# Attention: value products in two pairs a slot, key tiles 2 and 3 added into key tile 1 on GpSimd for the softmax denominator

## The chip, the cores and the metric

The kernel runs on one core of one Trainium2 chip. The metric is the device time of one execution in microseconds (us). The program is one launch of one decoder layer.

## What is computed

The input `x` is 4 sequences of 512 tokens, 512 wide, in float32. The layer has three parts, each followed by a residual sum and a layer norm: causal self-attention, a choice of one of four experts by token number, and a mixture of eight experts with a shared one. The change lies in the attention:

```
qkv = x @ w_attn + b_attn              # 16 heads of 32
att = softmax(causal(q k^T / sqrt(32)))
y   = (att @ v) @ w_proj + b_proj
x   = layernorm(x + y)
```

The softmax is divided at the end: the kernel keeps exp(score - rowmax), sums it over the keys, and multiplies the value product by the reciprocal of that sum.

## The kernel before

`attention_phase` treats 16 groups, 4 for each of the 4 sequences; a group g is four heads. All engines walk through one list of steps that `attention_steps` writes out by hand (line 24 on); each engine takes from it the kinds that concern it, in the list's order. So the list sets the order on TensorE (PE), GpSimd (POOL), ScalarE (ACT), VectorE (DVE) and SP alike. A pass of the loop over `s` (line 46) does the second half of group s, the first half of group s+1, the Q and K products of group s+2, and the value products of group s-1.

The steps, by their kind:

- Q, K, V, PR: products of the projections, each in three parts of four 128x128 by 512 matmuls (line 471), into one of two banks of `psT`. XT transposes x (line 485), CW transposes the weights of the next phase (line 492).
- The high and low halves of Q and K (`ch_hi`, ScalarE, line 613; `ch_lo`, VectorE, line 738) are stacked into `qS` and `kS` by 24 DMAs a group, nearly all from SP (line 354). ScalarE writes the next `ch_hi` of Q only when all stacks of the earlier groups have landed (line 612).
- P1 (line 537): scores of a unit, 10 units a group, two banks of `psS`; VectorE adds the mask and takes the row maximum (line 754). P1 of unit n waits for the maximum of unit n-2.
- M (line 545) turns the maxima into the layout of the exponent step.
- P2 (line 558): the scores transposed, keys on the partitions, less the maximum; ScalarE's exponential (line 641) writes unit u to `p_f[:, u, :]`, and GpSimd clears what is above the diagonal (`affine_select`, line 413). A unit is 512 columns. Units 0 to 3 hold key tile 0 of the four heads, units 4 to 7 key tile 1 (queries 128 to 511, 384 columns) and key tile 3 (queries 384 to 511, the last 128 columns), units 8 and 9 key tile 2 (256 columns for each head).
- PV(g, j) (line 562): for key tile j, four matmuls with the values into `psO` (one for each head, 32 columns of weights, beside each other in the array) and four with ones into `psN`, for the denominator. Both accumulate over j, in the order 0, 1, 3, 2. `pv_done` counts the tiles. A float32 matmul has two records in the trace.
- NORM (line 757): VectorE transposes `psN`, takes the reciprocal, transposes back and multiplies with `psO`. YH splits the result on ScalarE (line 648) and GpSimd (line 418).
- LN1 and LN2 (lines 433, 805) are the layer norm, ST the scatter to `sorted_x1` from GpSimd (line 441), LZ the load of the next z (line 448) and ZB its bias addition on GpSimd (line 427). LZ waits for all scatters so far (line 447).

In a pass, after Q, K and three P1, the loop of line 79 writes for each j: PV(s-1, j), one P1, one P2, and in the second pass of each sequence one of two XT. The rest of P1 and P2 follows, with the V or PR products spread between them. ScalarE's exponential of units 0, 4 and 8 waits until PV has read what it overwrites (line 640):

```
if u in (0, 4, 8) and g:
    act.wait_ge(pv_done, QT * (g - 1) + {0: 1, 4: 3, 8: 4}[u])
```

Of the kernel before, what the change touches and what calls it, by code (L numbers as in the profile page):

```python
# [13 lines left out]
ALU = mybir.AluOpType  # L14
# [3 lines left out]
P = 128  # L18
EPS = 1e-5
ONE = 1  # L20
BELOW_ALL = -1e30


def attention_steps(B, QT, NG):
# [13 lines left out]
    steps = []  # L38
# [7 lines left out]
    for s in range(NG):  # L46
        b, at = s // 4, s % 4
        fill, early, soon = [], [], []
# [3 lines left out]
        if at == 1:  # L52
# [3 lines left out]
            early = turn[:2]  # L56
# [16 lines left out]
        if not head:  # L73
            steps += p1[:2] + [("M", s)]
            p1 = p1[2:]
        else:
            p1 = p1[3:]
        if s:
            for n, j in enumerate(order):
                steps += [("PV", s - 1, j)] + p1[n:n + 1] + p2[n:n + 1] + early[n:n + 1]  # L80
                if s == NG - 2 and n < 2:
                    for i in (2 * n, 2 * n + 1):
                        steps += [("LN2", b - 1, i), ("ST", b - 1, i)]
                if s == NG - 1:
                    steps += [("ZB", b, n)]
                if n == 1 and at == 3 and b and b < B - 1:
                    steps += [("LZ", b)]
            p1, p2 = p1[4:], p2[4:]
        p2 = [x for pair in zip(p1, p2) for x in pair] + p2[len(p1):]
# [31 lines left out]
def attention_phase(nc, sems, acc, store, ident, powm, xs_in, pos, table, x, w_attn, b_attn, w_proj, b_proj, tokens, ctx_w, sorted_x1, sorted_x2):  # L121
# [28 lines left out]
    for s in steps:  # L150
        if s[0] in ("XT", "CW") or (s[0] in ("Q", "K") and s[-1] == 2):
            hi_order[s[:-1] if s[0] in ("Q", "K") else s] = len(hi_order)

    def first(s):
# [27 lines left out]
    with ExitStack() as ctx:  # L182
# [3 lines left out]
        def sem(name):  # L186
            return sems.enter_context(nc.semaphore(f"attn_{name}"))
# [87 lines left out]
        mask_done = sem("mask_done")  # L275
        pv_done = sem("pv_done")
        flip_done = sem("flip_done")
        norm_done = sem("norm_done")
# [93 lines left out]
        def _(pool):  # L372
# [32 lines left out]
            for s in steps:  # L405
                kind = s[0]
                if kind == "P2":
# [5 lines left out]
                    pool.affine_select(out=at, in_=at, compare_op=ALU.is_ge, fill=drop, base=0,  # L413
                                       pattern=[[0, at.shape[1]], [1, P]], channel_multiplier=-1).then_inc(mask_done, 1)
                elif kind == "YH":
                    g = s[1]
# [34 lines left out]
        def _(pe):  # L451
# [22 lines left out]
            for s in steps:  # L474
# [86 lines left out]
                elif kind == "PV":  # L561
# [3 lines left out]
                    if j == 0:  # L565
# [4 lines left out]
                        if g % 4 == 0:  # L570
                            for i in range(QT):
                                pe.wait_ge(sh_free[bank_of["V", g // 4, i]], use_of["V", g // 4, i] + 1)
                    for to, values in ((psO, lambda i: v_f[:, j, (g % 4) * P + i * D:(g % 4) * P + (i + 1) * D]), (psN, lambda i: ones[:])):
                        for i in range(4):
                            u, c0 = E_AT[j, i]
                            last = pe.matmul(to[i * D:(i + 1) * D, j * P:T], values(i), p_f[:, u, c0:c0 + (QT - j) * P],  # L576
                                             start=(j == 0), stop=(j == 2), tile_position=(0, i * D))
                    last.then_inc(pv_done, 1)

        @block.scalar  # L580
        def _(act):
# [3 lines left out]
            for s in steps:  # L585
# [47 lines left out]
                elif kind == "P2":  # L633
# [3 lines left out]
                    if u == 0 and g == 0:  # L637
                        act.wait_ge(w_lo_done, 5)
                    if u in (0, 4, 8) and g:
                        act.wait_ge(pv_done, QT * (g - 1) + {0: 1, 4: 3, 8: 4}[u])  # L640
                    act.activation(p_f[:, u, :], psE[:, n % 2, :], ACT.Exp, scale=SCALE).then_inc(exp_done, 1)  # L641
# [13 lines left out]
        def _(dve):  # L655
# [11 lines left out]
            for s in steps:  # L667
# [89 lines left out]
                elif kind == "NORM":  # L757
                    g, part = s[1:]
                    if part == 0:
                        dve.wait_ge(pv_done, QT * (g + 1))  # L760
                        dve.transpose(flip, psN[:]).then_inc(flip_done, 1)
# [10 lines left out]
                elif kind == "NH":  # L772
# [4 lines left out]
                    if half == 0:  # L777
                        dve.wait_ge(pv_done, QT * (g + 1))
                        dve.wait_ge(yl_done, g)
# [1193 lines left out]
```

## Time and profile before

| what | us |
|---|---|
| median of 3 runs | 1280.78 |
| lowest and highest of them | 1274.82 and 1282.97 |
| the profiled execution | 1269.57 |
| its span | 1267.7 |
| TensorE busy in it | 1183.1 (93%) |
| VectorE busy | 686.9 (54%) |
| ScalarE busy | 456.2 (36%) |
| GpSimd busy | 240.8 (19%) |

The durations of the rows come from the profiled execution; the 1.9 us between its time and its span lie around the first and last instruction. The attention takes the first third of the span, to about 450 us. Busy time of TensorE is counted from the start of a matmul to its modelled end, and matmuls overlap; the distance from one start to the next is what a matmul costs.

### The profile page before, as it was taken

Reading aid. Unit: us, or ns where it says so; the run is one execution under the profiler, and the core shown is the slowest. Engines: PE = TensorE matmul, PEld = TensorE weight load, DVE = VectorE, ACT = ScalarE, POOL = GpSimd, SP = SyncE. Lnnn points to the kernel's source line nnn. Section 1 sums busy time; section 2 is a strip of 40 time slices with the busy share of each in tenths; the row PEclk is TensorE's granted clock in tenths of the full one; section 3 lists DMA queues with packets and bytes.
Section 4 is the critical chain, followed back from the end, with each engine's and each line's share of the span. In section 5 each row is a group of like instructions: output and inputs, shape, how many; then the busy total and the mean of one; then the engine's idle time right before and its main releaser. Section 6 shows DMA issues by size and latency. Waiting matters only on the chain.

```text
span 1267.7 us, 20196 instructions
## 1 busy us (share of the span) xinstructions
PE 1183.1 (93%) x6404; PEld 935.7 (74%) x6404; DVE 686.9 (54%) x1469; ACT 456.2 (36%) x699; POOL 240.8 (19%) x370
## 2 busy tenths in 40 slices
PE   7788999999999879994999999999999999999996
PEld 5565676576575558883688888899999997778885
DVE  5564656656557546664447634343444442666744
ACT  3254435334435322222343334244444433333331
POOL 2021314413414410003100440000000000433200
PEclk8989999999999979997999999999999999999998
DMA  7336573532524222225223666245345531666440
GB/s 241 86 100 238 179 249 118 133 88 51 150 61 125 80 85 83 84 76 157 101 82 93 208 227 199 79 149 175 122 145 172 171 99 53 206 178 195 144 139 33
DMA packets 129277, 169.72 MB, mean 134 GB/s; under 512 B 17553, under 2 KB 70801, under 8 KB 129169
## 3 DMA queue, kind: packets, MB, share of 16 engines
q1 hardware_dynamic: 115360, 136.64, 35.2%
q0 software_dynamic: 8496, 28.32, 6.7%
q10 hardware_dynamic: 5312, 3.42, 1.2%
q8 instruction: 56, 0.92, 0.3%
q14 instruction: 53, 0.43, 0.1%
HBM read 95.98 MB, written 47.19 MB: 113 GB/s over the span
## 4 chain that ended last, share of the span: by engine, by line
PE 74%; DVE 8%; SPq 5%; POOL 3%; DMA 3%; issue 3%; ACT 2%; ACTq 1%; POOLq 0%; DVEq 0%
PE routed_ps L819 18%; PE routed_ps L1370 16%; PE psT L471 11%; SPq L354 5%; PE chosen_psG L819 4%; PE chosen_psY L819 4%; PE routed_ps L1389 2%; PE routed_ps L1390 2%; PE routed_ps L1391 2%; PE psS L537 2%; PE psO L576 2%; POOL routed_rows_io L1308 2%; PE psN L576 2%; PE psE L558 2%; PE routed_ps L1411 1%
## 5 line engine op out<-in xcount | busy, mean ns | idle before, releaser
L471 PE MATMUL psT<-store 128*128 128x512 f32 x576 | 157.2, 408 | 5.4 <-DVE store L685 3.5
L754 DVE CUSTOM_DVE_ANT_0 psS<-psS,attn_mask 128x512 f32<-128x512 f32 (+3 forms) x256 | 120.8, 510 | 60.3 <-PE psS L537 60.3
L641 ACT ACTIVATE acc<-psE 128x512 f32<-128x512 f32 x160 | 93.7, 599 | 141.7 <-PE psE L558 138.2
L1370 PE MATMUL routed_ps<-routed_later,routed_held 128*128 128x512 f32 x528 | 127.3, 398 | 3.6 <-issue 2.9
L1370 PE MATMUL routed_ps<-routed_first,routed_held 128*128 128x512 f32 x528 | 128.0, 396 | 1.4 <-DVE routed_first L1809 1.4
L471 PEld LDWEIGHTS psT<-store 128*128 128x128 f32 x576 | 105.7, 195 | 25.1 <-issue 4.0
L1370 PEld LDWEIGHTS routed_ps<-routed_later,routed_held 128*128 128x128 f32 x528 | 100.5, 192 | 28.0 <-DVE routed_held L1713 3.5
L819 PE MATMUL routed_ps<-routed_held,routed_h_hi 128*128 x624 | 116.1, 328 | 0.5 <-DVE routed_h_lo L1754 0.3
L1370 PEld LDWEIGHTS routed_ps<-routed_first,routed_held 128*128 128x128 f32 x528 | 99.7, 191 | 22.2 <-DVE routed_first L1809 1.8
L1308 POOL DMA_INDIRECT routed_rows_io<-sorted_y,routed_pos x32 | 37.6, 1175 | 387.8 <-DMA sorted_y<-routed_rows_io 314.0
L413 POOL TENSOR_SCALAR_AFFINE_SELECT acc<-acc 128x256 f32<-128x256 f32 (+1 forms) x160 | 57.2, 365 | 274.0 <-ACT acc L641 273.7
L819 PEld LDWEIGHTS routed_ps<-routed_held,routed_h_hi 128*128 128x128 f32 x624 | 100.4, 188 | 1.5 <-issue 1.3
L819 PE MATMUL routed_ps<-routed_first 128*128 x351 | 91.3, 404 | 0.0
L537 PE MATMUL psS<-attn_kS,attn_qS 96*128 96x512 f32 (+3 forms) x256 | 74.0, 352 | 12.2 <-DMA attn_kS<-attn_ch_hi 4.7
L537 PEld LDWEIGHTS psS<-attn_kS,attn_qS 96*128 96x128 f32 x256 | 44.6, 195 | 53.3 <-issue 22.8
L819 PEld LDWEIGHTS routed_ps<-routed_first 128*128 128x128 f32 x351 | 63.6, 190 | 12.2
L558 PE MATMUL psE<-attn_qS,attn_kS 100*128 100x512 f32 (+3 forms) x256 | 70.1, 339 | 2.2 <-ACT acc L641 2.1
L1713 DVE TENSOR_TENSOR routed_held<-routed_sraw,routed_held 128x1024 fp32r<-128x1024 f32 x44 | 53.8, 1222 | 29.5 <-ACT routed_held L1496 29.1
L1389 PE MATMUL routed_ps<-routed_held,routed_h_hi 128*128 128x512 f32 x176 | 68.8, 391 | 0.2 <-DVE routed_h_lo L1729 0.2
L1391 PE MATMUL routed_ps<-routed_held,routed_h_lo 128*128 128x512 f32 x176 | 68.5, 389 | 0.0
L1390 PE MATMUL routed_ps<-routed_held,routed_h_hi 128*128 128x512 f32 x176 | 68.5, 389 | 0.0
L1509 ACT ACTIVATE routed_h_f<-routed_ps 128x512 f32<-128x512 f32 x44 | 26.3, 598 | 115.1 <-PE routed_ps L1370 115.1
(249 smaller groups left out, 1973.8 us busy)
## 6 DMA issues: line engine op xcount, KB each, us to landing
sorted_x<-attn_zero SPq DMA_DIRECT2D x19, 768.0 KB, 5.9
routed_sraw<-in_L_ffn_Sg_dram SPq DMA_DIRECT2D x44, 256.0 KB, 3.1
routed_sraw<-in_L_ffn_Su_dram SPq DMA_DIRECT2D x44, 256.0 KB, 3.5
routed_sraw<-in_L_ffn_Sd_dram SPq DMA_DIRECT2D x44, 256.0 KB, 4.0
routed_rows_io<-sorted_x SPq DMA_DIRECT2D x39, 256.0 KB, 3.0
sorted_y<-routed_rows_io SPq DMA_DIRECT2D x39, 256.0 KB, 2.3
attn_qS<-attn_ch_hi SPq DMA_DIRECT2D x128, 64.0 KB
attn_kS<-attn_ch_hi SPq DMA_DIRECT2D x112, 64.0 KB
```

The lines of the kernel that those rows point to most:

```text
L354: sp.dma_start(dst[r * D:(r + 1) * D, i, :].bitcast(F32), part[i * D:(i + 1) * D, qk, :].bitcast(F32)).then_inc(stack_in, 16)
L471: last = pe.matmul(out, lhs[a](k), rhs[c](k), start=(s[-1] == 0 and k == 0), stop=(s[-1] == 2 and k == KC - 1))
L537: last = pe.matmul(psS[:, n % 2, c0:c0 + (t + 1) * P], q[0:AUX, i, t * P:(t + 1) * P], k[0:AUX, i, 0:(t + 1) * P], start=True, stop=True)
L558: last = pe.matmul(psE[:, n % 2, c0:c0 + (QT - j) * P], k[0:AUX + 4, i, j * P:(j + 1) * P], q[0:AUX + 4, i, j * P:T], start=True, stop=True)
L641: act.activation(p_f[:, u, :], psE[:, n % 2, :], ACT.Exp, scale=SCALE).then_inc(exp_done, 1)
L754: last = dve.tensor_tensor_reduce(scores, scores, mask[:, (3 - t) * P:T], 1.0, BELOW_ALL, ALU.add, ALU.max, rowmax[:, g % 2, t, i:i + 1])
L819: last = pe.matmul(out, lhs[a](k), rhs[c](k), start=(n == 0), stop=(n == 3 * chunks - 1))
L1308: pool.indirect_dma_start(out=got[:, n % 4, :], out_offset=None, in_=sorted_y, in_offset=bass.IndirectOffsetOnAxis(ap=pos[k][:, t:t + 1], ...
L1370: last = pe.matmul(out, w[:, slot, at + k * P:at + (k + 1) * P], x_part(k), start=(g == 0 and k == 0), stop=(g == 2 and k == KC - 1))
L1389: pe.matmul(s_y[i], h[0], w[0], start=(c == 0), stop=False)
L1390: pe.matmul(s_y[i], h[0], w[1], start=False, stop=False)
L1391: last = pe.matmul(s_y[i], h[1], w[0], start=False, stop=(c == CH - 1))
```

## The change

In the passes s = 1 to 14 (groups 0 to 13) the order changes: one more P1 goes first, PV of tiles 0 and 1 follow each other, then come four pairs of P2 and P1, then PV of tiles 3 and 2. Tiles 1, 3 and 2 have no matmuls with ones of their own any more. GpSimd adds tile 3 and then tile 2 into tile 1, in place, where their queries meet (AD 0 and AD 1), and one set of four matmuls with ones over the 384 columns of the sum (RS) accumulates it into `psN`. AD waits until PV has read tile 1, RS waits for both AD. The exponential of unit 4 waits for RS. Groups 14 and 15 stay as they were.

```diff
+def in_pairs(g, NG):
+    return g < NG - 2
...
+        joined = s and in_pairs(s - 1, NG)
+        if joined:
+            steps += p1[:1] + [("PV", s - 1, 0), ("PV", s - 1, 1), ("AD", s - 1, 0)]
+            p1 = p1[1:]
         if s:
             for n, j in enumerate(order):
-                steps += [("PV", s - 1, j)] + p1[n:n + 1] + p2[n:n + 1] + early[n:n + 1]
+                if joined:
+                    steps += p2[n:n + 1] + ([("AD", s - 1, 1)] if n == 0 else []) + p1[n:n + 1] + early[n:n + 1]
+                else:
+                    steps += [("PV", s - 1, j)] + p1[n:n + 1] + p2[n:n + 1] + early[n:n + 1]
...
+            if joined:
+                steps += [("PV", s - 1, 3), ("PV", s - 1, 2), ("RS", s - 1)]
             p1, p2 = p1[4:], p2[4:]
...
+    def pv_before(g):
+        return sum(QT + in_pairs(n, NG) for n in range(g))
+
+    def pv_all(g):
+        return pv_before(g + 1)
...
+                elif kind == "AD":
+                    g, part = s[1:]
+                    pool.wait_ge(pv_done, pv_before(g) + 2)
+                    if part == 0:
+                        pool.wait_ge(mask_done, UNITS * g + 8)
+                        at, more_p = p_f[:, 4:8, 2 * P:3 * P], p_f[:, 4:8, 3 * P:T]
+                    else:
+                        pool.wait_ge(mask_done, UNITS * (g + 1))
+                        pool.wait_ge(sum_done, 2 * g + 1)
+                        at, more_p = p_f[:, 4:8, P:3 * P], p_f[:, 8:10, :].rearrange("p u (h n) -> p (u h) n", h=2)
+                    pool.tensor_tensor(at, at, more_p, ALU.add).then_inc(sum_done, 1)
...
-                    for to, values in ((psO, lambda i: v_f[:, j, (g % 4) * P + i * D:(g % 4) * P + (i + 1) * D]), (psN, lambda i: ones[:])):
+                    kinds = [(psO, lambda i: v_f[:, j, (g % 4) * P + i * D:(g % 4) * P + (i + 1) * D]), (psN, lambda i: ones[:])]
+                    for to, values in kinds[:1] if in_pairs(g, NG) and j else kinds:
...
+                elif kind == "RS":
+                    g = s[1]
+                    pe.wait_ge(sum_done, 2 * (g + 1))
+                    for i in range(4):
+                        last = pe.matmul(psN[i * D:(i + 1) * D, P:T], ones[:], p_f[:, 4 + i, 0:3 * P], start=False, stop=True, tile_position=(0, i * D))
                     last.then_inc(pv_done, 1)
...
-                    if u in (0, 4, 8) and g:
-                        act.wait_ge(pv_done, QT * (g - 1) + {0: 1, 4: 3, 8: 4}[u])
+                    if u in (0, 4) and g and in_pairs(g - 1, NG):
+                        act.wait_ge(pv_done, pv_all(g - 1) if u else pv_before(g - 1) + 1)
+                    elif u in (0, 4, 8) and g and not in_pairs(g - 1, NG):
+                        act.wait_ge(pv_done, pv_before(g - 1) + {0: 1, 4: 3, 8: 4}[u])
...
-                        dve.wait_ge(pv_done, QT * (g + 1))
+                        dve.wait_ge(pv_done, pv_all(g))
```

## Rows read from the trace of the kernel before

**Rows 1.** Table of stretches: us; PE, PEld, DVE, ACT, POOL busy (count); PEclk, DMA share, GB/s
```profile
171.04:202.35 31.31, 30.11 (x193) 21.73 (x196) 20.52 (x58) 11.57 (x19) 6.96 (x15) 1.00 0.53 169
...
221.38:241.08 19.70, 17.94 (x129) 10.96 (x132) 11.34 (x38) 9.52 (x15) 11.70 (x20) 1.00 0.58 160
```
**Rows 2.** Timeline of SP's queue in slots 1 and 7: start us, us, what
```profile
93.02 3.74 SPq L324 DMA_DIRECT2D sorted_x<-attn_zero  x4
97.14 7.15 SPq L354 DMA_DIRECT2D attn_qS<-attn_ch_hi  x8
...
218.53 4.96 SPq L354 DMA_DIRECT2D attn_qS<-attn_ch_hi  x8
```
**Rows 3.** Chain of waits in slots 7 and 15: start us, us, what
```profile
233.12 3.44 DMA attn_kS<-attn_ch_hi
...
408.97 5.96 DMA attn_z<-in_x_dram
```
**Rows 4.** Timeline of TensorE in slot 8
```profile
241.01 1.07 PE L576 MATMUL psO<-acc 128*32 128x512 f32 x8
...
242.87 0.50 PE L537 MATMUL psS<-attn_kS,attn_qS 96*128 96x512 f32 x1
243.20 0.40 PE L558 MATMUL psE<-attn_qS,attn_kS 100*128 100x512 f32 x1
243.53 0.85 PE L576 MATMUL psO<-acc 128*32 128x384 f32 x8
244.20 0.83 PE L576 MATMUL psN<-acc,attn_ones 128*32 128x384 f32 x8
244.96 0.51 PE L537 MATMUL psS<-attn_kS,attn_qS 96*128 96x384 f32 x2
...
245.68 0.42 PE L576 MATMUL psO<-acc 128*32 128x128 f32 x8
245.92 0.40 PE L576 MATMUL psN<-acc,attn_ones 128*32 128x128 f32 x8
246.25 0.50 PE L537 MATMUL psS<-attn_kS,attn_qS 96*128 96x384 f32 x2
...
246.97 0.64 PE L576 MATMUL psO<-acc 128*32 128x256 f32 x8
247.43 0.61 PE L576 MATMUL psN<-acc,attn_ones 128*32 128x256 f32 x8
247.97 0.50 PE L537 MATMUL psS<-attn_kS,attn_qS 96*128 96x384 f32 x2
...
248.87 0.44 PE L471 MATMUL psT<-store 128*128 128x512 f32 x1
```
**Rows 5.** Groups of GpSimd's instructions, 60 to 430 us: busy us, mean ns, idle before
```profile
L413 POOL TENSOR_SCALAR_AFFINE_SELECT acc<-acc 128x256 f32<-128x256 f32 x96 | 38.3, 410 | 89.0 <-ACT acc L641 88.8
L427 POOL TENSOR_TENSOR attn_z<-attn_z,attn_bp 128x512 f32<-128x512 f32 x16 | 20.1, 1281 | 3.8 <-DMA attn_z<-in_x_dram 3.8
...
L413 POOL TENSOR_SCALAR_AFFINE_SELECT acc<-acc 128x128 f32<-128x128 f32 x64 | 18.9, 297 | 185.1 <-ACT acc L641 184.9
...
L433 POOL TENSOR_TENSOR attn_rstd<-attn_veps,powm 128x1 f32<-128x1 f32 x12 | 6.5, 550 | 1.4 <-DVE attn_veps L801 1.4
```
**Rows 6.** Timeline of GpSimd in slot 8
```profile
244.30 0.29 POOL L413 TENSOR_SCALAR_AFFINE_SELECT acc<-acc 128x128 f32<-128x128 f32 x1 [2.83 <-ACT acc L641]
```
**Rows 7.** Timeline of TensorE in slot 1
```profile
81.61 0.60 PE L485 MATMUL psT<-ident,attn_x_in 128*128 128x128 f32 x4
82.14 0.85 PE L576 MATMUL psO<-acc 128*32 128x384 f32 x8
```
**Rows 8.** Timeline of all engines in slot 14
```profile
393.44 1.27 POOL L418 TENSOR_TENSOR attn_yT_lo<-acc,attn_yT_hi 128x512 fp32r<-128x512 f32 x1
...
398.65 0.45 PE L558 MATMUL psE<-attn_qS,attn_kS 100*128 100x384 f32 x2
```
**Rows 9.** The operations of line 805: ns min/median/max, first and last start
```profile
L805 DVE TENSOR_SCALAR attn_z<-attn_z,attn_mv,attn_rstd x16: 528/542/1516, 215.0 to 443.8; 128x512 f32<-128x512 f32 x16
```

More of the change, by code:

```diff
@@ L276, in attention_phase @@
         pv_done = sem("pv_done")
+        sum_done = sem("sum_done")
         flip_done = sem("flip_done")
@@ L577, in _ @@
                                              start=(j == 0), stop=(j == 2), tile_position=(0, i * D))
+                    last.then_inc(pv_done, 1)
+                elif kind == "RS":
[3 more added lines that the diff above has]
+                        last = pe.matmul(psN[i * D:(i + 1) * D, P:T], ones[:], p_f[:, 4 + i, 0:3 * P], start=False, stop=True, tile_position=(0, i * D))
                     last.then_inc(pv_done, 1)
@@ L777, in _ @@
                     if half == 0:
-                        dve.wait_ge(pv_done, QT * (g + 1))
+                        dve.wait_ge(pv_done, pv_all(g))
                         dve.wait_ge(yl_done, g)
```

## Prediction

> **What bounds the kernel now.** I read the page first, then the table of stretches over the attention's slots, then the chain of waits and the queue of SP, and last the timeline of one slot. I call "slot s" the time from the first value product of group s-1 to that of group s; the change touches slots 1 to 14. The busy shares of the page are sums over stages with different limits, so the table of stretches decides: it parts the slots into two kinds [rows 1]. Slot 5 lasts 31.31 us and TensorE has 193 matmul records in it: it carries the fill (output projection, input transposes; slots 4, 8, 12 carry the V product). Slot 7 lasts 19.70 us with 129 records and no fill. The reader is to see that both show a granted clock of 1.00, so the difference is work, not clock.
>
> Slots without fill are not set by TensorE. SP issues the 24 stacking DMAs of a group one by one: eight of them take 4.96 us from 218.53 [rows 2], 0.62 each, so 24 take about 15 us; then the last one lands 3.44 us after 233.12 [rows 3], and only then may ScalarE write the next `ch_hi`. 15 + 3.4 + about 1.5 for `ch_hi` and `ch_lo` is the 19.7 us of slot 7. In the chain of waits this queue holds slots 2, 3 and 7, and likewise 11. Slots 6 and 10, in which the chain comes through VectorE's normalising at about the time the stack lands, I count with them. What TensorE saves there ends in a wait for the stack. So TensorE's time counts in slots 1, 4, 5, 8, 9, 12, 13 and 14 only: 8 of 14.
>
> **What is removed and added on TensorE.** The timeline of slot 8 gives each step by the distance of starts [rows 4]. Value product 0 (values and ones) takes 1.86 (241.01 to 242.87). Value product 1: values 0.67, ones 0.76. Product 3: values 0.24, ones 0.33. Product 2: values 0.46, ones 0.54. From the first to the first fill at 248.87 are 7.86 us, with five score steps (P1) and four exponent steps (P2) between. Removed are the ones of products 1, 3 and 2: 0.76 + 0.33 + 0.54 = 1.63. Added is RS, four products over 384 columns, the form of the ones of product 1: 0.76. Net 0.87 less in a slot, and the same P1 and P2. Without any wait a slot's section would end at 7.86 - 0.87 = 6.99, and RS would start at 6.23. Over 14 slots that would be 12.2 us; over the eight that count 7.0.
>
> **What is added on GpSimd, and the wait.** AD 0 adds 4x128 elements (512 a partition), AD 1 adds 4x256 (1024). The only GpSimd addition of two SBUF tiles here is that of z and the bias, 512 elements in 1281 ns [rows 5]. I take 1.28 for AD 0 and 2.5 for AD 1, 3.8 together, since it is the same operation on the same type. From below: at the slope of the masks, (410 - 297)/128 = 0.88 ns an element on a fixed 0.18 [rows 5], they would be 0.63 and 1.08, and RS would not wait. From above: the power of one element a partition takes 550 ns [rows 5]; if each of the four separate blocks paid that anew, each AD would grow by 1.65. The value taken is that of the nearest row; no row shows an addition in blocks.
>
> Timed from the slot's start: P1 goes ahead (0.33), product 0 to 2.19, the values of product 1 have ended at 2.19 + 0.85 = 3.04 [rows 4], AD 0 runs to 4.35. P2 of unit 0 starts at 2.86; its mask can start 1.10 later (243.20 to 244.30 [rows 4, 6]), so it is ready at 3.96 and waits for AD 0: to 4.65. AD 1 stands behind it in GpSimd's queue: to 7.15. RS is wanted at 6.23. TensorE, which works in order, waits 0.9 us and ends at 7.15 + 0.76 = 7.91 against 7.86 before. The whole saving is given back as a wait. Queued behind RS are P1 of unit 8 and P2 of unit 4, and ScalarE's exponent of unit 4, which would be 0.1 later; masks 1 to 3 behind AD 1 are not wanted before the next slot.
>
> By the Trainium skill, "GPSIMD Engine Reference", part on the measured `tensor_tensor` add, 2048 elements take 4497 ns; an estimate of 2.25 us for AD 1 from it would make this wait 0.65 instead of 0.9, 0.25 us a slot better. No row here has a GpSimd add longer than 512.
>
> **Slot by slot.** Slots 4, 8, 12, 13: +0.05 each, +0.2. Slots 5 and 9 have two transposes of x between the pairs (each 0.53 from start to start, 81.61 to 82.14 [rows 7]): RS is then wanted at 6.23 + 1.06 = 7.29, after AD 1 has ended, and the full 0.87 stays: -1.7. Slot 1 has them too, but its saving ends at SP: the clears occupy it until 93.02 + 3.74 = 96.76, and the next stacking DMA went out at 97.14 [rows 2], so at most 0.38 is gained: -0.35. The slots that SP holds: 0, and a saving's cover gone costs nothing there, as the extra wait is zero to 0.1. The normalisation (DVE) starts after one more maximum than before but has one less behind it: 0.
>
> Slot 14 is different. GpSimd's queue has the one-element powers and YH ahead of AD 0; YH starts at 393.44 and takes 1.27 [rows 8]. AD 0 is then 394.71 to 395.99, the mask to 396.3, AD 1 to 398.8, RS to 399.55. Before, the same work (through P1 of unit 6) was done at 398.65 [rows 8]. That is +0.9, and here the path goes on through YH to the load of z at 408.97 [rows 3], for which the last group's masks wait. Behind AD 1 on GpSimd stand the four scatters of x1 too (ST), which the load of z waits for; they go out later by at most the two adds, 3.8 us. Four scatters and the masks between them stood before between YH's end at 394.71 and the load at 408.97, mostly waiting for ScalarE's exponents, so I cost the delay at nothing; without that cover it is 1 to 3 us. In slots 7 and 11 GpSimd's load of z leaves up to 2 us later, and so do the bias additions behind it; the masks that stand behind those are of units 7 to 9 and are wanted by product 1 of the next slot at the earliest: 0, and up to 1 us each if the load lands late.
>
> Also in slot 14 VectorE's four normalising operations L805 (median 542 ns, longest 1516 [rows 9]) stand beside AD. The longest one is that beside YH at 393.44. I cost them at nothing: at worst one more is lengthened by 1516 - 542 = 0.97 us. The Trainium skill ("SBUF — State Buffer", section "Who interferes with whom") says that VectorE in a two-port mode and GpSimd lock each other out for a whole instruction; the lengthened operation agrees. By that rule the sum would be 1 us higher, all of it in slot 14, since a maximum reads only one operand from SBUF.
>
> Sum: -0.35 - 1.7 + 0.2 + 0.9 = -0.95, rounded -1.0 us. Durations come from the execution of 1269.57 us (span 1267.7 and 1.9 around it), which becomes 1268.6. The median of the runs shown is 1280.78, 0.9% above that execution; I carry the difference over: 1279.8.
>
> **Rivals.**
> 1. The additions are fast enough and RS never waits. For it: no GpSimd add in blocks of this form is shown. Against: 1281 ns for 512 elements. AD 1 would have to end by 6.23, so both adds in 2.9 us (6.23 - 3.04 - the mask's 0.3). Then slots 4, 5, 8, 9, 12, 13 gain 0.87 each, slot 1 0.35, slot 14 about 0: -5.6, 1275.2.
> 2. GpSimd becomes the bound and the kernel gets slower. One mechanism: AD 1 ends later, TensorE stands at RS. Each microsecond more in the two adds costs one in slots 4, 8, 12, 13 and 14 and, past 0.14, in 1, 5 and 9, so the sum turns positive where they take over 4.0 us together. With 1 us more: 4 x 1.05 + 0 in slots 1, 5 and 9 + 1.9, and 0 to 3 for the late scatters in slot 14: +6 to +9, say 1288. With the upper bound for blocks (3.3 us more): 4 x 3.35 + 3 x 2.3 + 4.2, and 2.5 each in slots 6 and 10, where the chain through VectorE would then come last: about +29, 1310. Against both is that the nearest row needs no block's price.
> 3. The queue of SP does not bound and all 14 slots gain: -12, 1268.8. Against it are the 3.44 us landing row and the 15 us of issue.
> 4. The time in RS is not the 0.76 of its form, or the tighter P1/P2 row makes VectorE's maxima the bound. P1 and P2 follow at 0.72 a pair (244.96 to 245.68), before and after; by up to 0.3 a slot, +2: 1283.
>
> **How the numbers follow.** Forecast 0.52, rival 1 0.16, rival 2 0.17 (0.05 of it the extreme), rival 3 0.04, rival 4 0.11. The predicted time is the forecast's, 1279.8. The range covers rivals 1, 3, 4 and the mild form of 2, with the scatter of the runs: 1268 to 1290; the forecast alone has 1276 to 1284. About 1% (12.8 us) is what a measurement of this kernel can tell from no change. Faster by over 1% needs rival 3 with luck: 0.05. Slower by over 1% needs the extreme of rival 2 or part of it: 0.08. Same: 0.87.
>
> **What would show it.** AD 0 near 1.28 and AD 1 near 2.5 us. TensorE idle before RS by 0.5 to 1.2 us, released by GpSimd, in slots 4, 8, 12, 13, about 2 in slot 14 and none in 1, 5 and 9. Slots 4 and 8 unchanged in length, slot 5 at 30.4, slot 7 at 19.7. In a slot, psN then has the matmuls of product 0 and of RS only: two forms instead of four. Wrong if RS finds its sum done in slots 4 and 8 (rival 1), if a stretch without fill gets shorter (rival 3), or if an AD 1 takes over 3 us (rival 2).

## The result, and the profile after

The changed kernel takes 1284.58 us in the median of 18 runs (1281.11 to 1289.77), the one before, in 18 runs beside it, 1276.8 (1267.97 to 1284.29). The ratio is 1.0052 with a 95% interval of 1.0035 to 1.0069: slower by half a percent, some 6.6 us. Forecast was 1.0 us less. The time lies within the range, and within 1% of before; the change was not neutral, though, and the mechanism that slows it stands in none of the terms.

The profiled execution took 1287.56 us. Its page, part 1 (busy time of each engine):

```profile
span 1285.7 us, 19790 instructions
...
PE 1180.5 (92%) x6180; PEld 936.9 (73%) x6180; DVE 685.6 (53%) x1469; ACT 455.0 (35%) x699; POOL 288.2 (22%) x398
```

TensorE is busy 2.6 us less and GpSimd 47 us more than before. Neither tells where the time went. The parts that the prediction priced come first. GpSimd's groups, 60 to 430 us, as [rows 5]:

```profile
L445 POOL TENSOR_TENSOR acc<-acc 128x1024 f32<-128x1024 f32 x14 | 33.4, 2385 | 0.0
...
L445 POOL TENSOR_TENSOR acc<-acc 128x512 f32<-128x512 f32 x14 | 17.9, 1281 | 75.3 <-PE psO L608 75.3
```

AD 0 takes 1.28 us, as the addition of z and the bias does, so four separate blocks cost nothing beyond their elements; AD 1 takes 2.39. All products of RS stand in the list of those who waited for the additions (us, times):

```profile
  PE psN L615: 3.6, 10
```

TensorE's matmuls of RS waited 3.6 us in 10 of 14 slots, 0.36 each: in none of slots 1, 5 and 9, as forecast, and not in slot 14 either, where about 2 us were. The timeline of TensorE in slot 6 shows why it is less than the 0.9 forecast (the last column is idle time before the instruction and what ended it):

```profile
207.67 0.51 PE L589 MATMUL psE<-attn_qS,attn_kS 100*128 100x512 f32 x1
...
208.53 0.45 PE L589 MATMUL psE<-attn_qS,attn_kS 100*128 100x512 f32 x1
...
209.38 0.86 PE L608 MATMUL psO<-acc 128*32 128x128 f32 x16
210.60 0.85 PE L615 MATMUL psN<-acc,attn_ones 128*32 128x384 f32 x8 [0.36 <-POOL acc L445]
```

The pairs of P2 and P1 follow at 0.86 and 0.85 us (207.67, 208.53, 209.38), not at the 0.72 of before (244.96 to 245.68 [rows 4]), so RS is wanted some 0.4 later than I timed it, and less is left to wait for. Experiment 3, which has no additions, shows the same 0.86, and 0.67 from the values of tiles 3 and 2 to RS, where this timeline has 1.22 (209.38 to 210.60): the wait costs 0.55 in a slot, of which the row shows 0.36 as idle.

The table of stretches, as [rows 1]: slots 4, 5 and 6, then slot 7 up to the transposes of its maxima and its end, then slots 13, 14 and 15.

```profile
145.51:173.66 28.15, 27.33 (x157) 19.64 (x156) 13.90 (x42) 9.70 (x15) 8.36 (x13) 1.00 0.65 213
173.66:203.98 30.32, 28.83 (x174) 21.35 (x173) 20.21 (x58) 11.47 (x19) 10.38 (x17) 1.00 0.53 174
203.98:222.97 18.99, 17.14 (x109) 10.54 (x108) 13.91 (x42) 9.39 (x15) 11.27 (x14) 1.00 0.42 114
222.97:240.18 17.21, 14.07 (x94) 8.29 (x93) 9.74 (x35) 7.17 (x13) 12.02 (x17) 1.00 0.60 170
240.18:244.85 4.67, 4.67 (x15) 3.38 (x15) 1.37 (x4) 2.23 (x2) 3.10 (x5) 0.63 0.34 84
374.42:398.45 24.03, 21.77 (x133) 15.10 (x132) 16.62 (x52) 8.48 (x13) 8.56 (x15) 1.00 0.38 102
398.45:417.06 18.61, 14.21 (x103) 9.01 (x102) 14.68 (x42) 8.31 (x17) 13.32 (x19) 0.91 0.35 110
417.06:430.38 13.32, 10.86 (x98) 5.75 (x97) 5.24 (x9) 10.10 (x18) 6.90 (x10) 1.00 0.47 162
```

I took the length of every slot in the same way from several profiles: three of the kernel before (the one read for the prediction and two more executions, 1278.22 and 1278.54 us) and two of the changed one (the second took 1282.68). Sums in us:

| slots | before, three profiles | mean | after, two profiles |
|---|---|---|---|
| 4, 5, 8, 9, 12 (fill) | 147.8, 147.9, 147.8 | 147.8 | 145.1, 145.1 |
| 1, 2, 3, 6, 7, 10, 11 (held by SP's stack at their end) | 141.4, 144.1, 144.8 | 143.4 | 147.0, 147.0 |
| 13, 14, 15 | 51.2, 51.3, 51.4 | 51.3 | 56.0, 56.2 |
| 1 to 15 | 340.4, 343.3, 344.0 | 342.6 | 348.0, 348.3 |

So three things happened: the fill slots won 2.8 us, more than forecast; the pass of group 13 lost 4.7; and the slots costed at nothing lost 3.6. Together +5.5, which is the measured loss within its interval. The middle row has a warning in it: the one profile that the prediction read was the shortest of the three by 2.7 us, and the three lie as far apart (3.4) as the loss is large. What differs between them are stretches with a low granted clock. I call such a stretch, with TensorE at 1.2 GHz instead of 2.4, a fall.

**Slot 14.** The chain of waits from the end of slot 13 on, where before P1 and P2 followed each other without a stop [rows 8]:

```profile
397.30 0.61 DVE psS L794
398.02 0.50 PE psS L568
...
402.48 2.95 DVE attn_z L845 x2
...
406.26 0.50 PE psS L568 x2
...
418.89 6.84 DMA attn_z<-in_x_dram
```

And the timeline of all engines there, the rows of the two stops:

```profile
397.14 0.15 DVE L841 TENSOR_SCALAR attn_veps<-attn_mv 128x1 f32<-128x1 f32 x1
...
398.02 0.50 PE L568 MATMUL psS<-attn_kS,attn_qS 96*128 96x512 f32 x1 [1.89 <-DVE attn_rowmax L794]
...
402.33 3.09 DVE L845 TENSOR_SCALAR attn_z<-attn_z,attn_mv,attn_rstd 128x512 f32<-128x512 f32 x2
...
402.63 2.51 POOL L445 TENSOR_TENSOR acc<-acc 128x1024 f32<-128x1024 f32 x1
...
406.26 0.50 PE L568 MATMUL psS<-attn_kS,attn_qS 96*128 96x384 f32 x2 [2.94 <-DVE attn_rowmax L794]
```

There are two stops of TensorE. The first, 1.89 us, falls just before value product 0: P1 goes ahead of it now, and its maximum stands in VectorE's queue behind the residual sums and layer norm statistics of LN1 (L833 to L841), the last part of the fill. Before, value product 0 came first, and its 1.86 us [rows 4] gave VectorE the time. The second, 2.94 us: two normalising operations of LN2 (L845) take 3.09 us instead of about 1.08, beside AD 1; P1 waits for a maximum behind them. The order alone, without any addition (experiment 2), has 0.86 us of wait at this same P1, so some 2.1 of the 2.94 come from the addition. The longest single one in the whole kernel went from 1516 to 2568 ns:

```profile
L845 DVE TENSOR_SCALAR attn_z<-attn_z,attn_mv,attn_rstd x16: 531/540/2568, 215.6 to 452.9; 128x512 f32<-128x512 f32 x16
```

It ends 0.28 us after AD 1 does (402.33 + 3.09 against 402.63 + 2.51). The Trainium skill ("SBUF — State Buffer", section "Who interferes with whom") says that the ports shared by the two are locked for a whole instruction; the trace agrees, by this end 0.28 us behind the addition's. After the second stop the granted clock falls in slot 14 (0.91 in the table); all three profiles of before have a fall in slot 14 too, later in it.

**The ends of slots 3, 7 and 11.** TensorE at the end of slot 7. First the timeline of the changed kernel:

```profile
238.62 0.50 PE L568 MATMUL psS<-attn_kS,attn_qS 96*128 96x512 f32 x1 [1.29 <-DMA attn_kS<-attn_ch_hi]
240.18 0.91 PE L576 MATMUL psT<-ident,attn_rowmax 128*4 128x128 f32 x4 [1.06 <-DVE attn_ch_lo L778]
240.75 2.05 PE L502 MATMUL psT<-store 128*128 128x512 f32 x4
...
243.03 1.43 PE L502 MATMUL psT<-store 128*128 128x512 f32 x4
...
244.85 1.06 PE L608 MATMUL psO<-acc 128*32 128x512 f32 x8
```

The same stretch of the kernel before, in the profile that the prediction read:

```profile
236.61 0.49 PE L537 MATMUL psS<-attn_kS,attn_qS 96*128 96x512 f32 x1 [0.55 <-DMA attn_kS<-attn_ch_hi]
238.18 0.60 PE L545 MATMUL psT<-ident,attn_rowmax 128*4 128x128 f32 x4 [1.07 <-DVE attn_ch_lo L738]
238.53 1.18 PE L471 MATMUL psT<-store 128*128 128x512 f32 x4
239.55 0.39 PE L537 MATMUL psS<-attn_kS,attn_qS 96*128 96x512 f32 x1
```

TensorE stands in two pieces, 0.55 + 1.07 before and 1.29 + 1.06 after. Behind it four products take 2.05 instead of 1.18 us: the stretch of 4.67 us has a granted clock of 0.63, so most of it ran at 1.2 GHz rather than 2.4. From those transposes to the next value product are 4.67 us against 2.83 (238.18 to 241.01 [rows 4]). This comes when SP's stack has landed, on the path. Both profiles of the changed kernel show a fall at the ends of 3, 7 and 11; of the three of before, one shows it at 3, two at 7, one at 11. All five have one more at the end of slot 1 or 2.

How long TensorE stands just before does not decide it. The changed kernel at the end of slot 3, and its stretch from the transposes of the maxima on:

```profile
139.31 0.50 PE L568 MATMUL psS<-attn_kS,attn_qS 96*128 96x512 f32 x1 [0.53 <-DMA attn_kS<-attn_ch_hi]
140.88 0.61 PE L576 MATMUL psT<-ident,attn_rowmax 128*4 128x128 f32 x4 [1.06 <-DVE attn_ch_lo L778]
...
140.88:145.51 4.63, 4.63 (x15) 3.39 (x15) 1.37 (x4) 2.21 (x2) 3.28 (x5) 0.63 1.05 408
```

The kernel before at the end of slot 11, where it stands longer and keeps the full clock:

```profile
335.58 0.50 PE L537 MATMUL psS<-attn_kS,attn_qS 96*128 96x512 f32 x1 [1.07 <-DMA attn_kS<-attn_ch_hi]
337.15 0.60 PE L545 MATMUL psT<-ident,attn_rowmax 128*4 128x128 f32 x4 [1.06 <-DVE attn_ch_lo L738]
...
337.15:339.98 2.83, 2.83 (x14) 2.06 (x14) 1.37 (x4) 1.99 (x2) 2.77 (x5) 1.00 0.28 70
```

Whether the fall needs TensorE to stand at all, and whether the change brings it more often, is what the experiments ask.

### The profile page after: what moved, and what is told of

Same layout as the page of the kernel before. It is cut to its first block, busy times and chain, and to the rows that moved or that the text cites. A ratio compares the mean times of both kernels' runs of the same rounds, so it can differ in the third digit from the quotient of the medians.

```text
span 1285.7 us, 19790 instructions
## 1 busy us (share of the span) xinstructions
PE 1180.5 (92%) x6180; PEld 936.9 (73%) x6180; DVE 685.6 (53%) x1469; ACT 455.0 (35%) x699; POOL 288.2 (22%) x398
## 4 chain that ended last, share of the span: by engine, by line
PE 68%; DVE 8%; SPq 6%; DMA 5%; POOL 4%; issue 3%; ACT 3%; ACTq 2%; another core or an unknown queue 1%; POOLq 0%; DVEq 0%
PE routed_ps L859 17%; PE routed_ps L1410 15%; PE psT L502 11%; SPq L374 5%; PE chosen_psG L859 4%; PE chosen_psY L859 4%; PE routed_ps L1429 2%; PE routed_ps L1431 2%; PE routed_ps L1430 2%; POOL acc L445 2%; PE psO L608 2%; PE psS L568 2%; POOL routed_rows_io L1348 1%; PE routed_ps L1451 1%; PE psE L589 1%
## 5 line engine op out<-in xcount | busy, mean ns | idle before, releaser
L502 PE MATMUL psT<-store 128*128 128x512 f32 x576 | 163.6, 422 | 4.0 <-DVE store L725 2.4
L502 PEld LDWEIGHTS psT<-store 128*128 128x128 f32 x576 | 110.7, 203 | 25.6 <-issue 3.0
L445 POOL TENSOR_TENSOR acc<-acc 128x512 f32<-128x512 f32 (+1 forms) x28 | 51.3, 1833 | 75.3 <-PE psO L608 75.3
```

What stands on the lines that cost most here:

```text
L445: pool.tensor_tensor(at, at, more_p, ALU.add).then_inc(sum_done, 1)
L502: last = pe.matmul(out, lhs[a](k), rhs[c](k), start=(s[-1] == 0 and k == 0), stop=(s[-1] == 2 and k == KC - 1))
```

## The experiments

Each ratio is to the kernel before, run beside it on the same chip. "Clock" is the granted clock, a mean over each run and over all runs of the kernel; the kernel before has 0.965 to 0.966, the changed one 0.962.

**1. Not in slots 3, 7 and 11.** Those have the old order.

```diff
-    return g < NG - 2
+    return g < NG - 2 and g % 4 != 2
```

> The change is undone in slots 3, 7 and 11 alone (groups 2, 6, 10). Theory: in the changed kernel the granted clock of TensorE falls to 0.5 at the end of these slots, and Q, K and M products before the next slot take 1.8 to 2.7 us more each time, 6.3 us in three. Then here the granted clock stays 1.00 at 4 and 8 and 12, each of slots 3, 7, 11 is 1.8 or more shorter than in the changed kernel, and the time is 5 to 7 us below it: ratio to before about 1.000. Rival (GpSimd's later z load and bias additions, or the stack's DMAs, lengthen these slots): the clock stays low somewhere or the slots stay long only where z is loaded, 7 and 11, and slot 3 is unchanged. Rival (the time is outside the attention): ratio stays 1.005.

Measured: 1.0023, 1.0001 to 1.0045, clock 0.964. Slots 3, 7 and 11 take 21.45, 22.37 and 21.91 us in its profile, and the clock still falls at the end of each, so the falls do not need the change inside these slots. The seven stack-held slots together are at 143.8 us all the same, where the changed kernel has 147.0 and before 143.4, and the ratio is 0.3% lower than the change's, where 0.4 to 0.5% was expected. So some of the loss in these slots goes with the change there, though the falls stay; one profile can't say more of it.

**2. The order alone.** All products with ones stay, no AD and no RS.

> The new order with P1 ahead and the value products in two pairs, but with all ones products in their place, no additions, no RS. Theory: TensorE's work is that of before, it does not stand at RS, and the clock stays 1.00 at the ends of slots 3, 7, 11; slot 13 still stands 1.9 us for the maximum that P1 ahead waits for (24.0 against 22.1), slot 14 is near that of before since no AD stands beside the normalising. Ratio to before 1.001 to 1.003. Rival (the order itself, through VectorE's maxima, costs the time): ratio 1.005 and the clock falls as in the changed kernel.

Measured: 1.0002, 0.998 to 1.0025, clock 0.966. Slots 4, 8 and 12 take 28.2 (before 28.4), slot 13 takes 24.13: the first stop is there without any addition. Slot 14 takes 16.39, with 0.86 us of wait where the changed kernel has 2.94. So the first stop belongs to the order, the second for the most part to the additions. The falls come at 2, 7 and 11, against the expectation that the clock would stay up at 7 and 11.

**3. No additions.** RS stays and does not wait; the denominators lack key tiles 2 and 3.

```diff
-            steps += p1[:1] + [("PV", s - 1, 0), ("PV", s - 1, 1), ("AD", s - 1, 0)]
+            steps += p1[:1] + [("PV", s - 1, 0), ("PV", s - 1, 1)]
...
-                    pe.wait_ge(sum_done, 2 * (g + 1))
```

> AD is left out and RS does not wait (the denominators then miss key tiles 2 and 3). TensorE has the changed kernel's work. It tells the wait for AD from the missing work. If the wait for the additions is what costs: slots 4, 8, 12 get 0.4 shorter than in the changed kernel (27.8), slot 14 about 1.9 shorter, and the clock does not fall at the ends of 3, 7, 11: ratio below 1.000, about 0.998. If the missing work (TensorE idle longer while it waits for the stack) lowers the clock: the falls at 3, 7, 11 stay, slot 14 is short, ratio about 1.002 to 1.003. The first is what the theory of a wait says, the second that of the missing work; I give the second 0.6.

Measured: 1.0001, 0.9976 to 1.0027, clock 0.963. Slots 4, 8 and 12 take 27.58 us against 28.14 after and 28.39 before. A slot could win 0.82; waiting for AD gives back 0.56 of it. Slots 5 and 9 stay at 30.33: no wait there, as forecast. The falls stay at 2, 3 and 7, and one comes at 10, so they do not need the wait for the additions. Slots 13 and 14 take 23.46 and 18.80: the first stop is there with its 1.89 us, the second is down to 0.85, but this profile has two falls in slot 14, so its length says nothing of the additions.

**4. P1 not ahead of value product 0.**

```diff
-            steps += p1[:1] + [("PV", s - 1, 0), ("PV", s - 1, 1), ("AD", s - 1, 0)]
-            p1 = p1[1:]
+            steps += [("PV", s - 1, 0), ("PV", s - 1, 1), ("AD", s - 1, 0)]
```

> The changed kernel without the one P1 ahead of the value products. Theory: slot 13 loses its 1.9 us idle before that P1 (the maxima stand behind the layer norm's steps on VectorE) and is 22.0 again; the other slots within 0.3; the falls of the clock stay. Time 2 us below the changed kernel, ratio to before 1.0035. Rival (P1 behind the pair costs it back, since VectorE has less to do during the value products): slot 13 short, but 0.3 more in each of the others, ratio 1.005.

Measured: 1.0038, 1.0014 to 1.0061. Slot 13 is back at 21.90, but slot 14 grows from 18.61 to 21.72. Timeline of VectorE, GpSimd and TensorE there:

```profile
398.71 4.61 DVE L844 TENSOR_SCALAR attn_z<-attn_z,attn_mv,attn_rstd 128x512 f32<-128x512 f32 x2
...
399.05 1.26 POOL L444 TENSOR_TENSOR acc<-acc 128x512 f32<-128x512 f32 x1
...
400.55 2.49 POOL L444 TENSOR_TENSOR acc<-acc 128x1024 f32<-128x1024 f32 x1
...
404.04 0.80 PE L567 MATMUL psS<-attn_kS,attn_qS 96*128 96x384 f32 x2 [4.35 <-DVE attn_rowmax L793]
```

Without the first stop LN2 meets both additions and takes 4.61 us, ending again 0.28 after the second of them (403.32 against 403.04). TensorE then stands for 4.35. Each stop hides part of the other.

**5. Ones of key tile 0 twice in slots 3, 7 and 11.** More work in TensorE's idle time, far ahead of the landing of the stack; the result does not change.

```diff
+                    if g in (2, 6, 10) and j == 0:
+                        for i in range(4):
+                            u, c0 = E_AT[j, i]
+                            pe.matmul(psN[i * D:(i + 1) * D, 0:T], ones[:], p_f[:, u, c0:c0 + T],
+                                      start=True, stop=True, tile_position=(0, i * D))
```

> The changed kernel, and in slots 3, 7 and 11 the four ones products of key tile 0 are done twice (the first result is overwritten), 0.98 us of TensorE's time in slots that the stack's DMAs hold. Theory A (the work taken from TensorE in the slots where it has to wait anyway lowers the granted clock behind them): the mean granted clock over the runs rises from 0.962 towards the 0.9655 of before, and the time falls by 1 to 3 us, ratio 1.003 to 1.0045, although work was added. Theory B (the clock falls by chance of where the idle stretches lie, the work does not matter): clock 0.962 and ratio 1.005 to 1.006.

Measured: 1.0037, 1.0018 to 1.0056, clock 0.964. The slots are 18.79, 21.89 and 21.24 us, with falls at 7 and 11 and none at 3. Ratio and clock lie where work added to idle time was expected to bring them, but the interval overlaps that of the change, so this didn't decide anything: the added work lies at the start of the slot, and TensorE still stands at its end.

**6. Not in slots 13 and 14.** `g < NG - 4`.

> The change is undone in slots 13 and 14 (groups 12 and 13). Theory: slot 13 goes from 24.0 back to 22.1 (TensorE stood 1.9 us for the maximum that the P1 ahead needs), slot 14 and 15 together from 31.9 back to 29.1 (AD beside the normalising, each blocking the other). Time 4 to 5 us below the changed kernel, ratio 1.0015 to 1.002; at the same granted clock it is level with before or 1 us below. Rival (the slots' delays are only shifted to the load of z at the end): 2 us or less.

Measured: 0.998, 0.9958 to 1.0001, clock 0.966. Slots 13 to 15 take 50.76 us; the loss there is gone, and the kernel is faster than the 1.0015 to 1.002 expected.

**7. Fill slots only.** `g < NG - 4 and g % 4 in (0, 3)`.

> The change stays only in slots 1, 4, 5, 8, 9 and 12, those with fill, where TensorE's time counts. Theory: slots 5 and 9 keep their 1.0 us each, slots 4, 8, 12 0.25 each, slot 1 0.3, the others are as before, and the granted clock is that of before: time 3 us below before, ratio 0.9975 (0.996 to 0.999). Rival (the clock is lower with less work in any slot): clock 0.963 to 0.964, ratio 0.999 to 1.001.

Measured: 0.9994, 0.9974 to 1.0014, clock 0.966; falls at 2, 7, 11 and 14. It keeps the gain of the fill slots (28.17, 30.09) and nothing else, and is no better than experiment 6. Slots 13 to 15 take 53.0 in its profile, 1.7 more than before, though nothing is changed in them, which again shows how far a single profile may lie off.

**8. Not group 13.** `g < NG - 3`: slot 14 alone has the old order.

> The change is undone in slot 14 alone (group 13); slot 13 keeps it. It divides the gain of leaving both out. Theory: slot 13 stays at 24.0 (the P1 ahead waits for a maximum that stands behind the projection's sum, the moments and the layer norm's steps), slot 14 goes back from 18.6 to 17.0 and slot 15 from 13.3 to 12.0, so the time is 3 to 4 us below the changed kernel, ratio 1.001 to 1.003. Rival (slot 13's 1.9 us is the whole loss, what slot 14 loses is made up before the load of z lands): ratio 1.004 to 1.005.

Measured: 0.9975, 0.9957 to 0.9992, clock 0.966. The table of stretches, slots 13, 14 and 15:

```profile
371.29:392.94 21.65, 21.27 (x132) 14.89 (x131) 14.36 (x41) 6.08 (x12) 6.65 (x11) 1.00 0.41 113
392.94:409.80 16.86, 14.17 (x119) 8.29 (x118) 15.99 (x54) 11.17 (x19) 11.70 (x21) 1.00 0.41 126
409.80:421.68 11.88, 10.85 (x98) 5.76 (x97) 4.15 (x8) 8.67 (x16) 6.93 (x10) 1.00 0.49 159
```

They sum to 50.4, against 51.3 before and 56.0 after. I had expected slot 13 to keep its 24 us; it doesn't, since the P1 that stands ahead of the value product belongs to the pass of group 13, though its wait falls into the slot before. Part of the 50.4 is that this profile has no fall in slot 14. This one line makes the change a gain of 0.25%.

Experiments 6 and 8 keep the change in all seven stack-held slots. Their profiles have falls at 2, 3, 7 and 11, as the changed kernel's, and sums of 146.2 and 146.4 us. But their mean clock, 0.966 over 12 runs each, is no lower than that of the kernel before, and the 0.9975 of experiment 8, some 3 us, is more than its slots 1 to 15 have won in the profile (342.1 us against 342.6). So the profiles say that the change brings more falls and costs some 3 us in these slots, and the means of the runs do not bear it out once group 13 is left alone. This stays open.

**9. LN2 and its scatters after RS in slot 14.** The mutual blocking alone is taken away.

```diff
-                if s == NG - 2 and n < 2:
-                    for i in (2 * n, 2 * n + 1):
-                        steps += [("LN2", b - 1, i), ("ST", b - 1, i)]
...
+            if s == NG - 2:
+                for i in range(QT):
+                    steps += [("LN2", b - 1, i), ("ST", b - 1, i)]
```

> The changed kernel, with the four normalising steps and scatters of slot 14 (LN2, ST) after RS, no longer beside AD. Theory (VectorE and GpSimd block each other there): the first two normalising operations take 0.54 each instead of 3.09 together, TensorE no longer stands 2.9 us for the maximum of P1 in slot 14, and slot 14 is 17 to 17.5 instead of 18.6; time 1 to 3 us below the changed kernel, ratio 1.003 to 1.0045. Rival (they are long for another reason, or the maxima behind them are then late by the same): slot 14 stays at 18.6 or more. A price that both share: the scatters go out 3 us later and the load of z waits for them.

Measured: 1.0005, 0.998 to 1.0031. Slot 14 takes 16.60 instead of 18.61. The chain of waits:

```profile
398.53 1.89 DVE attn_z L845 x4
...
410.22 7.46 DMA attn_z<-in_x_dram
```

Four operations of LN2 now take 1.89 us. Slot 13 keeps its 24.04 with the first stop, and slot 15 takes 13.52, where the load of z takes 7.46 us (5.96 before [rows 3], 6.84 after). That the later scatters are paid there was expected, but is not shown: the last scatter ends at 405.14, the load goes out behind YH at 410.22, and in experiments 1, 5 and 12, with group 13 changed too, the load takes 5.83 to 5.95. What lengthens it in some profiles stays open.

**10. TensorE kept busy while it waits for the stack, without group 13.** Transposes of the identity into `psO`, which is free then; nothing uses them. By the edit, and in the trace, 14 stand at the end of each of slots 3, 7 and 11 and 9 at the end of each of slots 2, 6 and 10. The expectation names the places wrongly (17 in each of these passes, and slots 4, 8 and 12).

```diff
+            busy = s >= 3 and at in (0, 3) and n == 3
-            steps += [one] + left[n:n + 1] + (p1[n - 3:n - 2] if n >= 3 else [])
+            steps += [one] + ([("DM", s, 8 if at == 0 else 3)] if busy else []) + left[n:n + 1] + (p1[n - 3:n - 2] if n >= 3 else [])
...
-                steps += [("M", s)]
+                steps += ([("DM", s, 6)] if busy else []) + [("M", s)]
...
+                elif kind == "DM":
+                    pe.wait_ge(norm_done, s[1] - 1)
+                    for _ in range(s[2]):
+                        pe.transpose(psO[:, 0:P], ident[:], ident[:])
```

> As the run that undoes group 13 alone (ratio 0.9975), and TensorE transposes the identity into psO (free then) while it would wait for the stack: 17 such transposes in each of the passes s = 3, 4, 7, 8, 11 and 12, in the last stretch of slots 3, 7 and 11 (14 of them) or of slots 4, 8 and 12 (fewer, 9). They compute nothing that is used. If it is the standing of TensorE before the stack lands that lowers its granted clock (theory): the rows of clock 0.50 at the ends of slots 3, 7 and 11 vanish, each of these slots is 2 to 3 us shorter (19.5 to 21 where they have 21 to 23.4), slots 4, 8 and 12 up to 0.9 longer, the mean granted clock is at 0.968 or above, ratio 0.990 to 0.996. If the clock falls there for another reason (rival): the falls stay, the ratio is 0.9975 to 1.001.

Measured: 0.9948, 0.9928 to 0.9967, clock 0.970, the fastest kernel of the study. The timeline of TensorE at the end of slot 7:

```profile
234.04 1.04 PE L529 MATMUL psO<-ident 128*128 128x128 f32 x8
235.82 0.51 PE L573 MATMUL psS<-attn_kS,attn_qS 96*128 96x512 f32 x1 [0.74 <-DMA attn_kS<-attn_ch_hi]
236.17 0.82 PE L529 MATMUL psO<-ident 128*128 128x128 f32 x6
237.39 0.60 PE L581 MATMUL psT<-ident,attn_rowmax 128*4 128x128 f32 x4 [0.40 <-DVE attn_ch_lo L783]
237.75 1.17 PE L503 MATMUL psT<-store 128*128 128x512 f32 x4
```

And the table of stretches from the P1 ahead of those transposes to the next value product:

```profile
236.17:240.46 4.29, 3.89 (x23) 2.83 (x21) 2.17 (x5) 3.11 (x4) 3.60 (x6) 1.00 0.20 48
```

The clock is granted in full, the four products take 1.17 us again, and from the transposes of the maxima to the next value product are 3.07 us (237.39 to 240.46) instead of 4.67. The falls are gone from the ends of 2, 3, 7 and 11, and slots 2, 3, 6, 7, 10 and 11 sum to 120.8 us against 126.1 without the transposes.

**11. The same transposes in the kernel before.**

> The kernel before with the same idle-time transposes. The kernel before shows the fall of the granted clock at about half of these places. If standing lowers the clock: no fall at the ends of slots 3, 7 and 11, mean granted clock 0.968 or above, ratio 0.995 to 0.998, and it is within 0.2% of the other kernel with these transposes. If the falls come for another reason: ratio 1.000 to 1.003, clock about 0.965. If only the changed order draws the falls to these places: this one 1.000 and the other below 0.996.

Measured: 0.9978, 0.9954 to 1.0002, clock 0.971; the kernel before beside it has 0.966. No fall at 3, 7 or 11 here either; the one that is left in slots 1 to 15 is at the end of slot 1, which has no transposes. So the falls at the stack's waits need TensorE's idle time in the old order too. The time's own interval just reaches no change; the clock and the two other runs with transposes carry the reading.

**12. The same transposes in the changed kernel, whole.**

> The changed kernel whole, group 13 included, with the idle-time transposes. They brought the kernel before to 0.9978 and the one without group 13 to 0.9948. If the change's loss is those two parts and no more (theory), taking the clock's part away leaves slots 13 to 15 at 56 (4.7 longer than before) and the gains of slots 1, 4, 5, 8, 9 and 12 (about 3.7): ratio 0.997 to 1.000, against 1.0052 without the transposes, no fall at the ends of slots 3, 7 and 11. If more is lost elsewhere in the changed kernel (rival): 1.002 or above.

Measured: 0.9995, 0.9967 to 1.0023, clock 0.968, where the change alone has 1.0052 and 0.962. The falls at 3, 7 and 11 are gone; slots 13 to 15 take 57.3 us (24.04, 20.83, 12.42). With and without group 13 the two kernels with transposes differ by 0.47%, or 6.0 us, and their slots 13 to 15 by 6.3 (57.3 against 51.0).

The closing sum: slots 1, 2, 3, 6, 7, 10 and 11 take 140.1, 141.0 and 141.4 us with the transposes (before, without group 13, changed), against 143.4 and 147.0 without them (before, changed). The changed kernel loses 1.3 us there instead of 3.6, so about 2.3 go with the falls. The 140.1 still has the fall at the end of slot 1 in it; over slots 3, 6, 7, 10 and 11 alone the loss is 4.1 without the transposes (104.86 against 100.73) and 2.2 with them (100.8 against 98.6), again 2 less. These are single profiles against a spread of 3.4 us, so 2 is an order of size. The ratios say that the transposes are worth 0.22% in the kernel before, 0.27% without group 13 and 0.57% in the whole change, each with an uncertainty of about 0.3. The rest of the loss I can't place: SP's 24 issues at slot 7 take 15.2 to 16.8 us from first to last, in some with one issue of 1.3 to 1.8 instead of 0.59 us, in the old order too.

## Why the prediction was right or wrong

- **What bounds the slots: right.** Two kinds, and the saving counts in the fill slots only. Without the transposes the stack-held slots sum to 143.0 to 147.0 us in the kernels with the change or a part of it, against 141.4 to 144.8 before: none won anything there.
- **RS saves 0.87, AD 0 1.28, AD 1 2.5: right.** 0.82 was measured in slots 4, 8 and 12 without the wait (28.39 to 27.58), about 1.0 in slots 5 and 9; the additions take 1.28 and 2.39. The bounds of the masks' slope and of the price for each block are both excluded; the nearest row was the right one. (By the recorded terms AD 0 ends at 4.32, not 4.35; nothing hangs on it.)
- **RS waits 0.9 in slots 4, 8, 12 and 13: mis-sized.** It costs 0.55, since the pairs of P2 and P1 ahead of it take 0.86 and not 0.72, a part of rival 4 that I had kept out of the sum. Given back was 0.56 of 0.82 instead of 0.9 of 0.87. The five fill slots won 2.8 us where -1.6 was forecast.
- **Slot 14, the late scatters and L805 both costed at nothing, L805 with "at worst" 0.97: the step that failed first.** The pass of group 13 was priced at +0.9 and cost 4.7 (51.3 to 56.0; undoing it alone: 50.4). Two terms were missing. P1 moved ahead of the value product was timed at 0.33 of its own, and not asked for what it waits: VectorE's queue there is full of LN1, 1.89 us. And LN2 beside AD, with P1's maximum behind it, was bounded by one more operation lengthened to 1516 ns. That row was read wrongly: the operation of 1516 ns starts at 215.42 in slot 6, beside a YH of 1.58 us; the one beside the YH of 1.27 at 393.44 took 1.43. Beside an addition of 2.51 us the operation took 2568 ns: the bound has to grow with the instruction that blocks. The rule of the Trainium skill ("SBUF — State Buffer", "Who interferes with whom"), weighed at +1 us, said as much, and I fed it the old duration. TensorE stood 2.94 us behind it, and the wait forecast at RS in slot 14, about 2 us, did not come. The late scatters are not shown to cost anything; the load of z took 6.84 and 6.88 us instead of 5.96 in the two profiles of the changed kernel, some 0.9 of the 4.7, but 5.83 to 5.95 in three other kernels with this pass changed.
- **Slots that SP holds, costed at 0: the step that failed second, less surely.** TensorE's spare time there was taken as free. In the profiles it costs 3.6 us in seven slots; about 2 of it goes with falls of the granted clock, in which Q, K and M, the work on the path behind the stack, run at half the clock. They are gone when TensorE is kept busy in its idle time. Why the change should have more of them is not shown: at slot 3 it stood shorter than before did without a fall, and the mean clock of experiments 6 and 8 shows no more of them. The one profile of before that I read showed fewer falls than the other two, so "both show a granted clock of 1.00" was true of it and not of the kernel.
- **Rival 2** ended on the right side by another mechanism. Its price, TensorE standing at RS past 4.0 us of additions, did not occur: they take 3.7 together.

## What to carry to other kernels

If TensorE waits in a stretch, and if its next work after the wait is on the path, look at the granted clock behind the wait in more than one profile before you call work taken off it there free, and consider filling the wait with matmuls that nothing needs (here -0.2% before the change, with an interval that just reaches 0, and -0.3 to -0.6% after it). When an instruction moves ahead, price the queue of the engine it waits for, at its new place. And when a long GpSimd operation is set beside VectorE's scalings, charge each one that starts beside it with that operation's whole duration, in the passes with a queue behind it; leave such a pass out if it is only one of fourteen.

## What the runs showed of the hardware

- GpSimd adds two float32 tiles at 1.28 us for 512 elements a partition and 2.39 for 1024, the 512 also in four blocks.
- A VectorE `tensor_scalar` of 128x512 (0.54 us) that meets such an addition ends 0.28 us after it: 2.57 us instead of 0.54 beside one of 2.51, and two of them take 4.61 us beside YH and both additions (experiment 4).
- TensorE standing for 1.29 and 1.06 us, 0.50 us of work between, was followed by 4.67 us at a granted clock of 0.63; so was 0.53 and 1.06 us at the end of slot 3 (4.63 us at 0.63). 1.07 and 1.06 us at the end of slot 11 before were not followed by a fall (1.00). The length of the stand alone does not tell.
- With transposes in the gap (standing 0.74 and 0.40 us at slot 7) none of the nine places at the ends of slots 3, 7 and 11 in three profiles had a fall. Without them the kernel before had it in four of nine and the changed one in six of six.
